# The rest contraction of layer 0 earlier in its chunk, layer 0's activations two steps earlier, and new places for the gathers

## What is computed

```
e = stack([tbl_f[ids[:, f]] for f in range(39)], axis=1)      # (2048, 39, 16)
x0, xk = e, e
for W, b in ((w0, b0), (w1, b1), (w2, b2)):                   # W: (39, fields of xk, 128)
    z = relu(einsum('bhd,bkd,hks->bsd', x0, xk, W) + b)
    xk, direct = z[:, :64], z[:, 64:]                         # the last layer: direct = z
logit = sum(concat(direct...), axis=-1)                       # (2048, 256)
h = relu(concat(logit, dense_ctx) @ W_top1 + b_top1)
y = relu(h @ W_top2 + b_top2) @ W_top3
```

## Time and profile before

| | us |
|---|---|
| median of 3 runs | 2592.86 (2591.3 to 2594.6) |
| the profiled execution | 2598.07 |
| its span, first to last instruction | 2596.2 |

### The profile page before, as it was taken

How to read it: one execution, slowest core, us unless ns; L and a number is a source line. 1 busy time by engine, 2 the same in 40 slices (tenths; PEclk the granted TensorE clock), 3 DMA queues, 4 the chain that set the end, 5 groups by cost and what they waited for, 6 DMA issues and landing times.

```text
span 2596.2 us, 32413 instructions
## 1 busy us (share of the span) xinstructions
PE 2443.5 (94%) x8654; PEld 1591.3 (61%) x8654; DVE 2169.6 (84%) x1872; ACT 1661.3 (64%) x2120; POOL 1875.1 (72%) x1270
## 2 busy tenths in 40 slices
PE   0899999999999999999999999999999999999989
PEld 0466666666656666666666666666666666666655
DVE  1588889889878888988988898898888888888880
ACT  1566666666666666766666676666666666666653
POOL 6578778777867777777787777778777777765450
PEclk6899999999999999999999999999999999999999
DMA  2677667667757766766776676677667666756730
GB/s 71 139 149 155 126 138 166 134 131 151 154 110 152 154 130 132 166 137 132 148 158 129 132 164 140 127 150 155 131 131 166 141 131 145 160 129 129 159 80 0
DMA packets 214715, 352.58 MB, mean 136 GB/s; under 512 B 34382, under 2 KB 47566, under 8 KB 214588
## 3 DMA queue, kind: packets, MB, share of 16 engines
q1 hardware_dynamic: 194717, 347.07, 61.6%
q0 software_dynamic: 19968, 5.15, 2.2%
HBM read 346.97 MB, written 5.12 MB: 136 GB/s over the span
## 4 chain that ended last, share of the span: by engine, by line
POOL 30%; issue 27%; PE 16%; DVE 9%; DMA 7%; ACT 7%; SPq 3%; POOLq 0%; ACTq 0%; DVEq 0%; another core or an unknown queue 0%
POOL emb L374 13%; POOL Pl L380 13%; DMA xb<-x_dram 7%; ACT Ph L514 5%; PE ps L807 5%; PE ps L797 4%; DVE P L692 3%; DVE ps L692 3%; PE ps L817 3%; POOL dir L404 3%; SPq L311 3%; DVE Pl L697 3%; PE ps L926 1%; PE ps L918 1%; POOL emb L385 1%
## 5 line engine op out<-in xcount | busy, mean ns | idle before, releaser
L380 POOL TENSOR_TENSOR Pl<-P,Ph 128x1024 fp32r<-128x1024 f32 x448 | 1072.3, 2397 | 479.1 <-ACT Ph L514 469.4
L692 DVE TENSOR_TENSOR P<-xb,ps 128x1024 f32<-128x1024 f32 x768 | 926.8, 1214 | 81.1 <-DMA xb<-x_dram 72.9
L807 PE MATMUL ps<-Ph,wh 128*128 128x512 f32 x1920 | 870.1, 459 | 8.1 <-ACT Ph L514 8.0
L697 DVE TENSOR_TENSOR Pl<-ps,Ph 128x1024 fp32r<-128x1024 f32 x512 | 626.1, 1223 | 178.9 <-ACT Ph L514 168.7
L374 POOL DMA_INDIRECT emb<-tbl_in,idx x624 | 601.0, 963 | 166.3 <-issue 145.3
L807 PE MATMUL ps<-Ph,wl 128*128 128x512 f32 x1792 | 707.4, 395 | 0.0
L514 ACT ACTIVATE Ph<-ps 128x1024 fp32r<-128x1024 f32 x512 | 523.3, 1022 | 285.3 <-DVE ps L692 217.3
L817 PE MATMUL ps<-Pl,wh 128*128 128x512 f32 x1920 | 689.7, 445 | 11.4 <-POOL Pl L380 11.3
L514 ACT ACTIVATE Ph<-P 128x1024 fp32r<-128x1024 f32 x448 | 474.6, 1059 | 325.3 <-DVE P L692 303.8
L692 DVE TENSOR_TENSOR ps<-xb,ps 128x1024 f32<-128x1024 f32 x512 | 628.2, 1227 | 28.1 <-DMA xb<-x_dram 10.2
L797 PE MATMUL ps<-P,wp 128*128 128x512 f32 x1280 | 603.7, 594 | 4.1 <-DVE P L692 4.1
(11 more groups left out here) (64 smaller groups left out, 826.7 us busy)
## 6 DMA issues: line engine op xcount, KB each, us to landing
xb<-x_dram SPq DMA_DIRECT2D x1280, 256.0 KB, 8.5
emb<-tbl_in,idx POOLq DMA_INDIRECT x624
x_dram<-rows_sb SPq DMA_DIRECT2D x64, 78.0 KB
xb<-w_in SPq DMA_DIRECT2D x15, 128.0 KB
xb<-wt_in SPq DMA_DIRECT2D x2, 512.0 KB, 8.6
xb<-dense_in SPq DMA_DIRECT2D x1, 768.0 KB, 5.9
wp<-w_in SPq DMA_DIRECT2D x5, 128.0 KB
xb<-w0a_in SPq DMA_DIRECT2D x1, 448.0 KB
```

What stands on the lines that cost most here:

```text
L380: pool.tensor_tensor(Pl[:, h_slot(ref, c, k)], P[:, p_slot(ref, c, k)], Ph[:, h_slot(ref, c, k)], ALU.subtract).then_inc(low_pool, 1)
L692: dve.tensor_tensor(p, xb[:, x], xk.unsqueeze(1).broadcast_to([128, 2, N]), ALU.mult)\
L697: dve.tensor_tensor(Pl[:, h_slot(ref, c, k)], p_ps, Ph[:, h_slot(ref, c, k)], ALU.subtract)\
L807: pe.matmul(z_of(c, k), w[:, q, j, :], Ph[:, h_slot(ref, c, k), j, :], start=k in (L1B, L2) and i + j == 0, stop=False)
```

## The change

- The rest set comes first: its sum at step 2, its two squares at step 5, `rest_low` at step 6 (now of the chunk c + 2 whose layer 0 is in hand), its matmul at step 9. The six full sets follow: sums at 5, 7, 9, 11, 13, 15, squares at 7, 10, 12, 14, 16, 18, contractions at 8, 10, 12, 14, 16, 18. Before, the full sets had sums from 3 to 13, squares from 6 to 16 and contractions from 6 to 16, and the rest 15, 18, 19, with `rest_low` at step 1 of the next chunk.
- `direct0`, `upper`, `lower` go from steps 2, 3, 4 to 0, 1, 2, and `direct2` from 5 to 4.
- The gathers get a list of steps for each of the four chunks (9, 10, 11 and 9 of them) and are issued one at a time at these; `next_ids` moves from the start of chunk 2 to step 18 of chunk 1; 13 instead of 12 gathers are issued ahead of the loop.
- `full_emb` goes from step 15 to 17 of chunk 1.

```diff
@@ -41,12 +41,12 @@
 PRING, HRING = 4, 5
 XSLOTS = PAIRS + PRE
 TRANSPOSE_AT, X2_AT = 0, 3
-SUM_AT = [3, 5, 7, 9, 11, 13, 15]
-SQUARE_AT = [6, 7, 10, 12, 14, 16, 18]
-CONTRACT_AT = [6, 8, 10, 12, 14, 16, 19]
-REST_AT = 1
-DIRECT0_AT, UPPER0_AT, LOWER0_AT, RELU2_AT, DIRECT1_AT, RELU1_AT = 2, 3, 4, 5, 7, 8
-HIGH_AT, FULL_AT, LOW_AT = 15, 15, 17
+SUM_AT = [2, 5, 7, 9, 11, 13, 15]
+SQUARE_AT = [5, 7, 10, 12, 14, 16, 18]
+CONTRACT_AT = [9, 8, 10, 12, 14, 16, 18]
+REST_AT = 6
+DIRECT0_AT, UPPER0_AT, LOWER0_AT, RELU2_AT, DIRECT1_AT, RELU1_AT = 0, 1, 2, 4, 7, 8
+HIGH_AT, FULL_AT, LOW_AT = 15, 17, 17
 FOLD0A_AT, FOLD0_AT, FOLD1A_AT, FOLD1_AT = 14, (12, 14, 16, 18), 8, (6, 8, 10, 12)
 FOLDS = 5
 COL1 = (0, 1, 0, 2)
@@ -56,7 +56,9 @@
 SINGLE_STEPS = [k for k in range(STEPS) if (k + PRE if k < L1B else k - L1B if k < L2 else k - L2) == SINGLE // 2]
 assert all(k in SPL for k in SINGLE_STEPS)
 CHUNKS = TILES * CPT
-GATHER_AT = [k for k in range(STEPS) if KIND[k] != "G"]
+NEXT_IDS_AT = (1, 18)
+GATHERS = [[1, 2, 3, 5, 9, 14, 16, 17, 18], [1, 2, 3, 5, 6, 8, 9, 10, 18, 18],
+           [1, 2, 3, 5, 6, 9, 10, 12, 14, 16, 17], [1, 2, 3, 5, 6, 8, 9, 10, 17]]
 
 
 ORDER = [(-1, k) for k in range(L1B, L2)] + [(i, k) for i in range(CHUNKS) for k in range(STEPS)
@@ -421,7 +423,7 @@
                 take_ids(T)
 
             next_ids(1)
-            early = 12
+            early = 13
             for f in range(early):
                 gather(f)
             for k in range(L1B, L2):
@@ -430,19 +432,18 @@
 
             def tile(T, ref, fields, first=False, last=False):
 
+                todo = [list(f) for f in fields]
                 for c in range(CPT):
-                    if c == 2 and fields[c]:
-                        next_ids(T + 2)
-                    todo = list(fields[c])
-                    slots = [k for k in GATHER_AT if c != 1 or k < FOLD0A_AT - 4]
                     for k in range(STEPS):
                         if KIND[k] == "G" and (CPT * ref + c, k) in STEPSET:
                             low(T, ref, c, k)
-                        if k in slots:
-                            n = -(-len(todo) // len(slots[slots.index(k):]))
-                            for f in todo[:n]:
-                                gather(f)
-                            todo = todo[n:]
+                        if (c, k) == NEXT_IDS_AT and todo[2]:
+                            next_ids(T + 2)
+                        part = min(c, 1) if (c, k) < NEXT_IDS_AT else 2
+                        n = GATHERS[c].count(k) * (1 + (first and c == 0))
+                        for f in todo[part][:n]:
+                            gather(f)
+                        todo[part] = todo[part][n:]
                         if c == 0 and not first and k in FOLD1_AT:
                             if k == FOLD1_AT[0]:
                                 pool.wait_ge(z2_read, T * CPT)
@@ -462,13 +463,15 @@
                         if c == 1 and k == LOW_AT and not last:
                             low_emb(T + 1)
 
-            cuts = (0, 12, 21, 30, NF)
-            third, fourth, first, second = (range(a, b) for a, b in zip(cuts, cuts[1:]))
-            tile(0, 0, (range(early, 30), range(30, NF), third, fourth), first=True)
+            late, soon = len(GATHERS[0]), len([k for k in GATHERS[1] if (1, k) < NEXT_IDS_AT])
+            cut = NF - late - soon
+            assert sum(map(len, GATHERS)) == NF
+            start, middle, rest = range(0, cut), range(cut, cut + late), range(cut + late, NF)
+            tile(0, 0, (range(early, cut + late), rest, start), first=True)
             with pool.Fori(1, TILES - 2) as T:
-                tile(T, 1, (first, second, third, fourth))
-            tile(TILES - 2, TILES - 2, (first, second, (), ()))
-            tile(TILES - 1, TILES - 1, ((), (), (), ()), last=True)
+                tile(T, 1, (middle, rest, start))
+            tile(TILES - 2, TILES - 2, (middle, rest, ()))
+            tile(TILES - 1, TILES - 1, ((), (), ()), last=True)
             pool.wait_ge(z2_read, chunks)
             for stage in range(1, FOLDS):
                 fold1(TILES - 1, stage)
@@ -498,12 +501,13 @@
 
             def square(T, number, t):
                 act.wait_ge(aux_ready, T * PER["aux"] + number + 1)
-                if t < FULL0:
-                    act.activation(sq[:, t % 2, :], aux_ps, ACT.Square).then_inc(aux_read, 1)
-                else:
-                    act.activation(sqx[:, :], aux_ps[0:REST0], ACT.Square).then_inc(rest_high, 1)
-                    act.wait_ge(rest_high, T * CPT + number // AUX + 1)
-                    act.activation(aux_ps[LAST_LO], aux_ps[LAST_LO], ACT.Square).then_inc(rest_square, 1)
+                act.activation(sq[:, t % 2, :], aux_ps, ACT.Square).then_inc(aux_read, 1)
+
+            def rest_squares(T, number):
+                act.wait_ge(aux_ready, T * PER["aux"] + number + 1)
+                act.activation(sqx[:, :], aux_ps[0:REST0], ACT.Square).then_inc(rest_high, 1)
+                act.wait_ge(rest_high, T * CPT + number // AUX + 1)
+                act.activation(aux_ps[LAST_LO], aux_ps[LAST_LO], ACT.Square).then_inc(rest_square, 1)
 
             def round_(T, ref, c, k):
                 act.wait_ge(products, upto(T, ref, STEP, c, k))
@@ -535,8 +539,9 @@
                 if g:
                     act.wait_ge(rows_written, 16)
                 copy_x(0, AUX * g)
-                for t in range(T0):
-                    square(0, AUX * g + 1 + t, t)
+                rest_squares(0, AUX * g + 1)
+                for t in range(1, T0):
+                    square(0, AUX * g + 1 + t, t - 1)
                     s = t - (T0 - PRE - 1)
                     if g and 0 <= s < PRE and KIND[L1B + s] != "P":
                         round_(0, 0, -1, L1B + s)
@@ -572,7 +577,10 @@
                             copy_x(T, aux)
                         if k in SQUARE_AT and not no0:
                             t = SQUARE_AT.index(k)
-                            square(T, aux + 1 + t, t)
+                            if t:
+                                square(T, aux + 1 + t, t - 1)
+                            else:
+                                rest_squares(T, aux + 1)
                         if c == 1 and not last:
                             if k == HIGH_AT:
                                 high_emb(T + 1)
@@ -706,6 +714,8 @@
             dve.wait_ge(xk1_ready, 1)
             waiting = None
             for s in range(PRE):
+                if s == 1:
+                    rest_low(0, 1)
                 dve.wait_ge(xb_in[s], 32)
                 product(0, 0, -1, L1B + s)
                 if waiting:
@@ -713,7 +723,6 @@
                 waiting = (0, 0, -1, L1B + s) if KIND[L1B + s] == "V" else None
             if waiting:
                 low(*waiting)
-            rest_low(0, 1)
 
             def tile(T, ref, first=False, last=False):
                 for c in range(CPT):
@@ -736,8 +745,8 @@
                         if waiting:
                             low(*waiting)
                         waiting = (T, ref, c, k) if KIND[k] == "V" else None
-                        if k == REST_AT and not end and not (first and c == 0):
-                            rest_low(T, c + 1)
+                        if k == REST_AT and not (last and c >= 2):
+                            rest_low(T, c + 2)
                         if end and k == L2 + 5:
 
                             dve.wait_ge(mlp_high, 2)
@@ -778,15 +787,17 @@
 
             def sums(t):
 
-                rows = R0 if t < FULL0 else REST0
+                rows, t = (R0, t - 1) if t else (REST0, FULL0)
                 pe.matmul(aux_ps[0:rows], sel[:, t, 0:rows], x2[:, :], start=True, stop=True)\
                     .then_inc(aux_ready, 1)
 
-            def contract0(t, bank):
-                if t < FULL0:
-                    pe.matmul(z0_ps[:, bank], w0[:, t, :], sq[:, t % 2, :], start=t == 0, stop=False)
+            def contract0(t, bank, start, stop):
+                if t:
+                    m = pe.matmul(z0_ps[:, bank], w0[:, t - 1, :], sq[:, (t - 1) % 2, :], start=start, stop=stop)
                 else:
-                    pe.matmul(z0_ps[:, bank], w0x[:, :], sqx[:, :], start=False, stop=True).then_inc(squares_done, 1)
+                    m = pe.matmul(z0_ps[:, bank], w0x[:, :], sqx[:, :], start=start, stop=stop)
+                if stop:
+                    m.then_inc(squares_done, 1)
 
             def z_of(c, k):
                 return z1_ps[:, c % 2] if k < L1B else z1_ps[:, (c + 1) % 2] if k < L2 else z2_ps
@@ -858,11 +869,11 @@
                     pe.wait_ge(aux_read, number + 1 + t)
                     sums(t)
                     if t:
-                        contract0(t - 1, g)
+                        contract0(t - 1, g, t == 1, False)
                     if g and t >= T0 - PRE:
                         late = contract(0, 0, -1, L1B + t - (T0 - PRE), late)
                 pe.wait_ge(aux_read, AUX * (g + 1))
```

(8 more changed lines are left out.)

## The result

| | us |
|---|---|
| before, median of 4 runs | 2592.26 (2591.3 to 2594.6) |
| after, median of 4 runs | 2673.1 (2670.24 to 2673.48) |
| ratio after / before | 1.0308, 95% interval 1.029 to 1.0326 |
| after, the profiled execution | 2673.18, span 2671.1 |

A forecast was written before the change was run, and what follows sets the result against it. TensorE, busy for 94%, paced chunks at 37.91 us, with a recurring wait at L789 for `rest_low`. The ring of 39.16 adds 1.25 times 61, 76 us: 2598.07 + 76 - 5.2 = 2669 us, range 2600 to 2700.

The forecast's parts named there:

- (a): Rest contraction to step 9, `rest_low` to step 6: removes TensorE's 1.0 us wait and 0.69 us of VectorE work.
- (b): Full squares' contractions two steps later: the 0.86 us covering `direct1` and the rounding goes, so TensorE waits before high(7).
- (c): `direct0` on ScalarE waits for the last square contraction, holding the next chunk's roundings 0 and 1: over 2 us later.
- (d): `rest_low` at step 6 frees the accumulator bank: TensorE's step 5 sum waits about 1.6 us, plain(5) and low(4) behind.
- the ring: From high(7) through last contraction, `direct0`, roundings, products, `rest_low`, low(4) to next high(7): 39.16 us per chunk; chance 0.72.
- TensorE's own time: Rival: neither `rest_low` nor `squares_done` ends last, TensorE alone decides: 37.43 us per chunk, 2564 us; chance 0.11.
- the ring over the loads: Rival: ScalarE's hold doesn't bind; product 10 to product 4, `rest_low`, low(4), product 10: 37.62 to 38.63, 2606 us; chance 0.12.
- (e): New gather places on GpSimd, beside broadcast loads that fill the DMA and delay product 4 by 1.01 us: priced at nothing.
- The cover named: Product 4 reached at 986.84, 0.4 after its loads allowed it; without that a chunk could win or lose 1.01 us.
- (f): `full_emb` copy two steps later on ScalarE, 64% busy: nothing, or less than 15 times one activation of 1.06 us.
- The clock: Rival: two TensorE pauses per chunk bring its clock down once per tile, 50 us on top, 2719; chance 0.05.
- The sum: Profiled time before 2598.07, plus 76 over 61 chunks, minus 5.2 from profiled to plain median: 2669 us.

The follow-up runs named there:

- product 10 first: Step 8's low part behind product 10 on VectorE: against the kernel before 2534.7 us; with `rest_low` at step 0 and the new gather places too, 2516.83 us.

## Why the prediction was right, and where not

- **(a), the wait at L789 goes:** right. The run with `rest_low` at step 0 shows it was a true loss and could be had for less.
- **(b), the cover of `direct1`:** right. 0.86 had been worked out as exposed. The profile has 0.69 idle in front of high(7) at 1020.84, to which the modelled end of the matmul before adds some; with half loads and `direct0` back, where nothing else waits, the pace was 37.39, against 37.43 worked out with the 0.86.
- **(c) and (d), the ring:** right in its place and, link by link, in its size, 39.16 against 39.12. The forecast for TensorE's wait at the sum, 1.6 us, was too high: 65.4 us in 61 times, 1.1 each. Part of the difference is the modelled end of the matmul before: by starts, TensorE stands for 1.23 (the low part at 1014.61 occupies 0.46). The rest, 0.4, had been lost earlier in the same stretch, at the sum of the rest set and at high(4), which at 1013.58 already waited for rounding 4. Together that is the 1.6.
- **What the ring was compared with:** this step was weak. The prediction put TensorE's own time at 37.43 and the ring over the loads at 38.13, where it measured 38.83. I had worked out 38.63 from one chunk and then gone half way down to 37.62, as if the 1.01 us that product 4 waited for its load were a cost that could vanish. With full loads it doesn't: the way from product 10 to product 4 has a median of 25.2 us in before and of 25.5 in the run with `direct0` back, single chunks between 24.1 and 26.9. Nor is the wait in front of product 4 the whole of it: with `direct0` back product 2 waits for a load as often, and without waits for loads the way is 23.0, 2.5 shorter. At 38.63 the rival would have said 2637, at the measured 38.83 it would have said 2649, and it would have been seen that `direct0` back brings little.
- **(e), the gathers:** priced at nothing, worth about 6 us in the kernel before, through the one late gather; that is 0.1 us per chunk, within the 1.01 that had been named. The cover named was missing in the kernel before, where product 4 waited for its load in 56 of 60 chunks, and is there in the changed one, where it did so in 6. What the new places are worth in the changed kernel no run shows; with `direct0` back it was 3.4 us, within the uncertainty.
- **(f), the copies:** priced at nothing from ScalarE's share of busy time, worth 7 to 8 us in the kernel before. The share is a mean over the chunk; at step 15 two copies stood ahead of a rounding for which VectorE waited, and VectorE's work was the ring there. The bound named, 15 times 1.06, held.
- **The clock:** the mean granted clock of after was 0.996, of before 0.984. Two pauses in each chunk didn't bring it down; that rival is out.
- **The sum:** 2598.07 + 76 - 5.2. The profiled run of after was not 5.2 above its median but level with it, so the last term had no place there: the 39.16 for every chunk had already replaced the long chunk of before. Without it the forecast would have been 2674.

## What to carry to other kernels

A wait in an in-order queue costs what stands behind it. Before moving an instruction ahead of others, follow the ring from its wait back to itself through all engines, and sum it link by link from rows: that gave the pace of a chunk here to 0.05 us. Then do the same for the next longest ring, with every matmul that waits on the way in it, since what an edit brings or costs ends at the second ring. And price a transfer by the time from its release to its arrival, never by the wait that is seen in front of it. Nor is an engine's share of busy time slack for a copy: look at what stands behind it in its own step.

## What the runs showed that I had not expected

- The DMA, full for 21 us of the chunk looked at the earlier trace rows, sets a distance that hardly moves: from the first product that frees a slot to the product that needs the ninth pair of loads the medians are 25.2 to 25.5 us in the seven kernels where that product waits for a load in nearly every chunk, with paces from 37.2 to 38.9 (25.8 in the two with product 10 first). In the changed kernel the same distance, 25.6, is the ring of ScalarE's hold: with half loads it stays.
- With loads of half the columns the kernel with `direct0` back lost all its waits for loads, and its pace fell by 1.44 us: a kernel whose TensorE is busy for 92% was paced by its DMA, through a wait of about 1 us on another engine.
- Changes of 1.5 to 3.5% came from moving one instruction by a step or two: 39 us from `rest_low`, 60 from the low part of step 8; 90 the other way from `direct0` and what follows it, moved by two.
- A copy of 1.3 us on ScalarE, which was busy for 64%, cost 0.5 us each time, as a rounding stood behind it; and a gather that came late in old and new places alike cost 6 us only where five gathers stood in a row ahead of a low part.
